# Second attention of a two-layer conditioned sequence model: q stacked by DMA like k, scores of two heads as two row-half matmuls

## The reference, cut to what matters

```python
x_mod = _modulate(_ln(x), shift_msa, scale_msa)      # layer norm, scale and shift by the condition
k, q, v = jnp.split(x_mod @ w_qkv, 3, axis=-1)        # each 256 x 256, seen as 256 tokens x 16 heads x 16
q = q / CH
w = jax.nn.softmax(jnp.einsum('bqhc,bkhc->bhqk', q, k), axis=-1)
y = jnp.einsum('bhqk,bkhc->bqhc', w, v).reshape(B, S, H)
x = x + gate_msa[:, None] * (y @ w_proj + b_proj)
```

## Time and profile before

| | us |
|---|---|
| time, median of two runs | 1826.03 (1824.8 and 1827.25) |
| span of the profiled execution, first to last instruction | 1819.8 |
| what the median has more than this span | 6.2 |

### The profile page before, as it was taken

How to read it: one execution, slowest core, us unless ns; L and a number is a source line. 1 busy time by engine, 2 the same in 40 slices (tenths; PEclk the granted TensorE clock), 3 DMA queues, 4 the chain that set the end, 5 groups by cost and what they waited for, 6 DMA issues and landing times. The chain is left out here.

```text
span 1819.8 us, 46726 instructions
## 1 busy us (share of the span) xinstructions
PE 1757.5 (97%) x15198; PEld 1633.4 (90%) x15198; DVE 1340.7 (74%) x3119; ACT 944.7 (52%) x2099; POOL 362.4 (20%) x470
## 2 busy tenths in 40 slices
PE   7999989999999969999999999999998899999998
PEld 7999989999999967888888888888886899999998
DVE  4888876666666647888888888888885677777776
ACT  2666653333333345777676777777776333333332
POOL 2233331222122200111111111111111212221221
PEclk8999989999999989999999999999999799999999
DMA  7300010000000002111111111111110111111111
GB/s 215 127 20 20 20 33 1 0 0 0 0 0 0 0 14 72 52 49 50 48 48 48 48 48 48 48 48 49 49 49 27 50 47 46 35 46 46 46 42 39
DMA packets 73579, 73.97 MB, mean 41 GB/s; under 512 B 13489, under 2 KB 63985, under 8 KB 73537
## 3 DMA queue, kind: packets, MB, share of 16 engines
q1 hardware_dynamic: 70928, 73.31, 12.9%
q10 hardware_dynamic: 2448, 0.08, 0.1%
q0 software_dynamic: 160, 0.04, 0.0%
HBM read 38.62 MB, written 8.55 MB: 26 GB/s over the span
## 5 line engine op out<-in xcount | busy, mean ns | idle before, releaser
L1418 DVE TENSOR_REDUCE C_negmax<-bank 128x2 f32<-128x512 f32 x512 | 340.2, 686 | 101.1 <-PE bank L1226 98.1
L1338 ACT ACTIVATE C_probs<-bank 128x512 f32<-128x512 f32 x512 | 301.3, 598 | 139.2 <-PE bank L1238 134.4
L1226 PE MATMUL bank<-C_kx,C_qs 128*128 128x256 f32 x1024 | 217.9, 295 | 5.1 <-DMA C_kx<-C_k_hi 2.6
L892 ACT ACTIVATE D_g<-bank,D_bias 128x256 f32<-128x256 f32 x256 | 107.6, 472 | 221.3 <-PE bank L181 221.3
L1238 PE MATMUL bank<-C_qs,C_kx 128*128 128x256 f32 x1024 | 221.2, 298 | 0.1
L892 ACT ACTIVATE B_g<-bank,B_bias 128x256 f32<-128x256 f32 x256 | 107.6, 472 | 218.5 <-PE bank L181 193.1
L1226 PEld LDWEIGHTS bank<-C_kx,C_qs 128*128 128x128 f32 x1024 | 156.2, 189 | 33.3 <-issue 17.7
L1238 PEld LDWEIGHTS bank<-C_qs,C_kx 128*128 128x128 f32 x1024 | 155.9, 189 | 29.0 <-ACT C_probs L1338 15.6
L181 PE MATMUL bank<-D_wt_w_hi,D_g_lo 128*128 128x256 f32 x512 | 147.3, 288 | 6.0 <-DVE D_g_lo L920 4.6
L181 PE MATMUL bank<-B_wt_w_hi,B_g_lo 128*128 128x256 f32 x512 | 145.7, 285 | 5.2 <-DVE B_g_lo L920 5.0
L181 PE MATMUL bank<-B_h_hi,B_wt_w_lo 128*128 128x256 f32 x512 | 147.4, 288 | 1.9 <-DVE B_h_lo L294 1.9
(11 more groups left out here) (265 smaller groups left out, 5218.0 us busy)
## 6 DMA issues: line engine op xcount, KB each, us to landing
C_kx<-C_k_hi SPq DMA_DIRECT2D x256, 64.0 KB, 2.6
C_kx<-C_k_lo SPq DMA_DIRECT2D x128, 64.0 KB, 2.6
C_gbc<-mod_rows SPq DMA_DIRECT2D x32, 256.0 KB, 3.2
D_gbc<-mod_rows SPq DMA_DIRECT2D x32, 256.0 KB, 3.4
out<-xres SPq DMA_DIRECT2D x32, 256.0 KB, 3.5
xres<-in_x SPq DMA_DIRECT2D x4, 1792.0 KB, 16.6
A_orow_bc<-mod_rows SPq DMA_DIRECT2D x32, 128.0 KB, 2.9
stage<-in_L_cond_mlp_w SPq DMA_DIRECT2D x2, 1024.0 KB, 12.5
```

Of the source, the lines that this page charges most:

```text
L892: ins = eng.activation(g[u][:, d * S:(d + 1) * S], hbank[u][:, d * S:(d + 1) * S], func, bias=per_seq(bias1, 2 * u + d, b))
L1226: ins = eng.matmul(sbank[h % 2][:, qh * S:(qh + 1) * S], qs[b.par][:, t * S + qh * P:t * S + (qh + 1) * P], kx[b.par][e][:, t * S:(t + 1) ...
L1338: e_exp.by(eng.activation(probs[h % NP][:, :], stbank[h % 2][:, :], ACT.Exp, scale=scl))
L1418: e_max.by(eng.tensor_reduce(n3[:, :, col], sbank[h % 2][:, :].rearrange("p (q k) -> p q k", q=TH), AX, ALU.max, negate=True))
```

## The change

* q is permuted like k (the weights of q too), and its high and low parts go into qs by DMA: `place` issues 6 DMAs of 64 KB for each half w of the heads, for q as for k. `Q_SLOTS` is (hi, hi, lo), `K_SLOTS` (lo, hi, hi). The selection tiles, SQ0 to SQ3, and the moves on ACT are gone.
* kx is one tile for each parity, with both halves filled; a score matmul reads 48 rows (50 for the transposed scores) of one half. A task is now a pair of heads: 4 matmuls, alternating between the halves and the two banks. A pair waits until both maxima (exponentials) of the pair before are taken.
* q0, k0 wait for lo_q, lo_k; q1 and k1 wait for task v of their sequence. hi_q waits until all 24 DMAs of the sequence before have landed; hi_k no longer waits for DMAs.
* The tables have new slots; PEEL is 6, MAX_SKEW 4, and the first input load keeps its 4 sequences (X_FIRST).

```diff
-PEEL = 4
+PEEL = 6
+X_FIRST = 4
...
-        SLOTS, MAX_SKEW = 16, 3
+        SLOTS, MAX_SKEW = 16, 4
...
-                K_SLOTS = ("hi", "lo", "hi")
-                K_DMAS = 2 * len(K_SLOTS)
...
-                kx = [[sb(f"kx{u}{e}", [P, NT * S], F32R) for e in range(2)] for u in range(UNROLL)]
+                Q_SLOTS, K_SLOTS = ("hi", "hi", "lo"), ("lo", "hi", "hi")
+                ROWS = len(K_SLOTS) * CH
+                STACK_DMAS = 2 * (len(Q_SLOTS) + len(K_SLOTS))
...
+                kx = [sb(f"kx{u}", [P, NT * S], F32R) for u in range(UNROLL)]
...
+                            for n in "qk":
+                                w_raw, s_in = raw_qk[n]
+                                eng.wait_ge(s_in, 16)
...
+                                        ins = eng.tensor_copy(d4, s5[:, :, :, :, e])
...
-                T_PE = {"T": -0.5, "q": 3, "k": 6.5, "v": 16.5, "SQ0": 8.5, "SQ1": 12, "SQ2": 13, "SQ3": 14.5,
-                        "M0": 25.5, "M1": 33, "AV0": 38, "AV1": 41, "AV2": 46.5, "AV3": 49.5, "Y1a": 45, "Y1b": 52,
-                        "Y2": 55, "PR": 59}
...
+                T_PE = {"T": -0.5, "q": 5.5, "k": 8, "v": 16.5, "M0": 26.5, "M1": 34.5, "AV0": 39, "AV1": 42.5,
+                        "Y1a": 47, "AV2": 47.5, "AV3": 51, "Y1b": 54, "Y2": 57, "PR": 61}
+                T_ACT = {"hi_h": 0.5, "hi_q": 6.5, "hi_k": 9, "v": 18, "M0": 27, "M1": 35, "Y0": 43.5, "Y1": 52,
+                         "hi_y": 58}
+                T_DVE = {"stats": -3.5, "xhat": -2, "lo_h": 1.5, "lo_q": 8.5, "lo_k": 10, "M0": 27.5, "M1": 35.5,
+                         "Y1a": 48, "Y1b": 55.5, "lo_y": 59, "out": 62}
...
-                T_S, T_ST = {h: 16 + h for h in range(NH)}, {h: 32.5 + h for h in range(NH)}
...
+                T_S, T_ST = {f"S{t}": 18 + 2 * t for t in PAIRS}, {f"ST{t}": 33.5 + 2 * t for t in PAIRS}
+                T_MAX, T_EXP = {t: T_S[f"S{t}"] + 0.5 for t in PAIRS}, {t: T_ST[f"ST{t}"] + 0.5 for t in PAIRS}
...
-                            e_max.wait(eng, b, h - 1)
+                        def scores(b, t):
+                            if t % 4 == 0:
+                                eng.wait_ge(s_st[t // 4][b.par], (b.pair + 1) * STACK_DMAS * 16)
+                            e_max.wait(eng, b, 2 * t)
                             for qh in range(TH):
...
+                                for e in range(2):
+                                    rows = slice(e * HALF, e * HALF + ROWS)
+                                    ins = eng.matmul(sbank[e][:, qh * S:(qh + 1) * S],
+                                                     qs[b.par][rows, t * S + qh * P:t * S + (qh + 1) * P],
+                                                     kx[b.par][rows, t * S:(t + 1) * S], start=True, stop=True)
+                                    if qh == TH - 1:
+                                        e_s.by(ins)
...
                         def hi_q(b):
-                            e_sq.wait(eng, b.back(1))
-                            hi_bias(b, "q", qk["q_hi"], bias_q, e_q, e_hiq)
-
-                        def hi_k(b):
                             prev = b.back(1)
                             if not prev.before_first():
                                 for w in range(2):
-                                    eng.wait_ge(s_kst[w][prev.par], (prev.pair + 1) * K_DMAS * 16)
+                                    eng.wait_ge(s_st[w][prev.par], (prev.pair + 1) * STACK_DMAS * 16)
+                            hi_bias(b, "q", qk["q_hi"], bias_q, e_q, e_hiq)
...
-                        def place_k(b, w):
...
+                        def place(b, w, name, stacked, slots, e_lo):
...
                             if w == 0:
-                                e_lok.wait(eng, b)
+                                e_lo.wait(eng, b)
                             else:
-                                e_sqev.wait(eng, b)
+                                e_v.wait(eng, b)
                             for e in range(2):
-                                for slot, part in enumerate(K_SLOTS):
+                                for slot, part in enumerate(slots):
...
-                        T_SP = {"k0": 10, "k1": 21.5, "M0": 26, "M1": 38.5, "gates": 41}
...
+                        T_SP = {"q0": 9.5, "k0": 12, "q1": 17.5, "k1": 21, "M0": 28, "M1": 36, "gates": 41}
```

More of the change, by code:

```diff
@@ L231, in stats @@
                 if x_in is not None:
-                    s, dmas = x_in[0 if b.reg is None and b.off < PEEL else 1]
+                    s, dmas = x_in[0 if b.reg is None and b.off < X_FIRST else 1]
                     eng.wait_ge(s, 16 * dmas)
@@ L1117, in _ @@
-                            ins.then_inc(s_mmk, 1)
+                            for n in "qk":
+                                eng.wait_ge(s_perm[n], 1)
+                                for t in range(KT):
+                                    for k in range(KT):
+                                        ins = eng.matmul(pshift[n][:, t * NB:(t + 1) * NB],
+                                                         w_perm[n][:, k * D + t * P:k * D + (t + 1) * P],
+                                                         shift1a[:, k * NB:(k + 1) * NB], start=k == 0, stop=k == KT - 1)
+                                ins.then_inc(s_mmb[n], 1)
@@ new lines, in scores_t @@
+                        def scores_t(b, t):
+                            if t % 4 == 0:
+                                eng.wait_ge(s_mdma[t // 4][b.par], (b.pair + 1) * MAX_DMAS * 16)
+                            e_exp.wait(eng, b, 2 * t)
+                            for kh in range(TH):
+                                for e in range(2):
+                                    rows = slice(e * HALF, e * HALF + ROW_LO + 1)
+                                    ins = eng.matmul(stbank[e][:, kh * S:(kh + 1) * S],
+                                                     kx[b.par][rows, t * S + kh * P:t * S + (kh + 1) * P],
+                                                     qs[b.par][rows, t * S:(t + 1) * S], start=True, stop=True)
+                                    if kh == TH - 1:
+                                        e_st.by(ins)
@@ L1432, in lo_bias, with lo_q, maxima @@
                             e_out.by(ins)
-                        def lo_k(b):
+                        def lo_q(b):
                             e_st.wait(eng, b.back(2), 8)
-                            lo_bias(b, "k", qk["k_hi"], qk["k_lo"], bias_k, e_hik, e_lok)
+                            lo_bias(b, "q", qk["q_hi"], qk["q_lo"], bias_q, e_hiq, e_loq)
+                        def maxima(b, t):
+                            for h in (2 * t, 2 * t + 1):
+                                maximum(b, h)
                         def y_norm(b, w):
```

198 lines of the change are left out of this document (67 added, 131 removed).

## The result

The changed kernel takes 2175.57 us (median of 2174.45 and 2176.69) against 1826.03: 1.191 of the time before, 95% interval 1.188 to 1.195, so 349.5 us slower. The forecast was 1948 us, in a range from 1885 to 2005: the direction was right, the size far off. The profiled execution has a span of 2174.8 us.

What follows compares the result with a forecast made beforehand. PE bounded the kernel before, at 22.41 us a sequence; a circle of waits (25.7 us, plus 0.6 for the clock) would replace it. 31 x (26.3 - 22.41) = 121, plus 1.2 prelude: 1826 + 122 = 1948 us, range 1885 to 2005.

Steps and rivals of the forecast that it cites:

- Step 1: ACT, DVE, SP: hi_q then lo_q end 1.95 us after the last k1 DMA lands; q0, k0 issue from there.
- circle: Waits closing over one sequence, from landed DMAs through hi_q, DVE, v and q1 to the next landing: 25.7 us.
- step 4: DVE: xhat waits for POOL's rstd (0.82 us), then xhat 1.33, out 0.76, maxima of pair 6 1.29.
- Step 6: SP: q1 waits 3.6 us for v, then q1, M1, k1 issues and landing take 11.0 us.
- SP's price: SP: each q DMA issue costs 0.64 us like k's; a half of six with its gap takes 3.93 us.
- rival 4: PE: row halves may not overlap but run one after the other; 6 us each way; no chance given.
- rival 3: PE falls to 1.2 GHz every period, mode changes add: 28 us or more, about 2001 us; chance 0.20.
- Rival 1: PE's relief comes through: a period near 20 us, 1752 us; chance 0.03.

Runs made afterwards that it cites:

- run 2: The changed kernel with POOL's two residual additions taken one iteration sooner; 1940.88 us.
- run 4: The kernel before with MAX_SKEW 4 (and with it POOL's lag), PEEL 6 and `out` moved past stats; 2039.87 us.
- run 3: As run 2, with q1 and k1 no longer waiting for v, and M1 behind k1 on SP; 1874.16 us.
- run 10: As run 6, with q made one place sooner on PE, ahead of the transposed scores of pair 2; 1789.51 us (0.980).
- run 7: The kernel before with row halves alone in the score matmuls, still one head at a time; 1896.68 us (1.040).
- run 5: As run 3, with two copies of q_hi, q_lo, k_hi, k_lo, hi_q waiting for DMAs of two sequences before; 1873.47 us (1.026).
- run 6: As run 5, with xhat behind the maxima of pair 6 on DVE and out, T, hi_h later; 1838.08 us (1.008).
- run 8: As run 5, with DVE's list laid out anew, stats half an iteration earlier; 1883.91 us (1.030).
- run 9: As run 8, but with one copy of q_hi, q_lo, k_hi, k_lo; 1882.94 us (1.029).

## Why the prediction was right or wrong, point by point

* **Step 1 failed**: "q0 and k0 are issued from here". The step looked at the semaphore that q0 waits for, and not at what stands ahead of q0 on SP, the gates load, with a wait of its own on POOL. q0 starts 10.3 us after lo_q's end (1026.16 to 1036.49), not at once. In the first sequences, where the gates load does not wait yet, rstd rows stand at 706.56, 733.08 and 760.73 us, 26.5 and 27.7 apart, where 26.3 was forecast. Run 2 takes POOL's lag away and lands 7 us from the forecast; run 4 puts it with the later `out` into the kernel before and costs 218 us.
* That run 2 lies only 7 us from the forecast is in part luck. Its circle has the forecast's parts: lo_q, M0, the wait at q1, the landing, and the clock at 0.5 in each period (for 3.4 us in most). But 31 steps of 25.75 - 22.41 us give 104 and not 121 us; xhat took 0.73 us where 1.33 was forecast. The fill ahead of the first rstd (668.06 us, before 664.38) and all that comes behind the last (1453.47 of 1939.0 us, before 1345.81 of 1819.8) give some 15 us where 1.2 was forecast for the prelude and nothing for fill and drain.
* Behind step 1 stand two rows of the change that were read as neutral: MAX_SKEW 4, which is also POOL's lag, and `out` "62" behind "stats" and "xhat". The prediction quotes DVE's new order, and in step 4 uses it for a sum of durations, but doesn't ask who takes C_tmp, and when POOL passes.
* **Step 4** also lacked the wait of `out` for POOL, 1.4 us, since rstd and both additions stand one behind the other on POOL. Its 0.82 us for rstd were nearly right (0.91).
* **Step 6**: in the profile after, q1 doesn't wait for v, as SP comes to it so late. In run 2 it does, 3.9 us against 3.6; in run 3 it goes, and 2.1 us of a period with it.
* **SP's price** was right: six issues of q take 3.91 us with the gap behind them (1022.15 to 1026.06 in run 2), as k's took 3.93, and by the profile page after they land 2.5 to 2.6 us behind their issue.
* **Row halves**: rival 4 is out. PE's timeline of run 10:

```profile
1004.76 0.51 PE L1218 MATMUL bank<-C_qs,C_kx 50*128 50x256 f32 x4
1005.11 0.40 PE L1205 MATMUL bank<-C_kx,C_qs 48*128 48x256 f32 x4
1005.44 0.39 PE L180 MATMUL bank<-C_h_hi,C_wq_lo 128*128 128x256 f32 x1
```

  Four matmuls on alternating halves take 0.33 us from their start to the full-height matmul behind them (1005.11 to 1005.44), with 0.1 us for the change of shape in it, where four full-height ones take 0.48 (0.12 each). PE's need is 185.09 us in 200 us of run 10, or 19.2 us a sequence; the forecast took 19. Its "some tenths of a microsecond" for a change of shape were more than its rows said (0.20 - 0.12 = 0.08 us ahead of the products with v); run 7 has 0.1 us on either side.
* **The clock** (rival 3 gave 2001 us for it): after the change PE is at the 1.2 GHz level for 14 to 17 of 34 us in nearly all periods, but as a follower of SP's stall: in run 2, with the gates load in time, it is there for 3.4 us in most periods, and the period is 25.75. What the low clock by itself adds to the 34 us, no run separates. In runs 3, 5, 6, 8 and 9 a fall, behind an idle stretch of 1.3 us where rival 3 had 2.6, makes the sequence in which it comes some 1.4 to 1.5 us longer.
* **Rival 1**, PE's relief, does exist: 1789.5 us in run 10, against 1752 worked out. The way there took four things that the change didn't bring: POOL's addition in time, q1 without v, rstd hidden, and q where PE waited. They were added one on the other, and no run leaves one of the earlier ones out at the end.

## What to carry to other kernels

For a wait on a queue that works in order, list what stands ahead of the instruction too: one small DMA with a wait of its own, which cost nothing while it was always met, can hold up all that is put behind it. When a task is moved past another in one engine's list, look for the engine that takes its output at a fixed point of the iteration: put behind that point, the output is taken an iteration later (30 us here). Where several limits lie close together, opening one may show nothing until the next is found. And a mean period can hide two kinds of sequences: sort them by the granted clock before a gain is put down to the clock.

## What the runs showed of the hardware that was not expected

xhat is the same instruction in all runs, and takes twice as long beside POOL's additions as with POOL at rest. The groups of DVE from 800 to 1300 us (count, busy us, mean ns, idle before), after:

```profile
L268 DVE TENSOR_SCALAR C_xhat<-xres,C_mv,C_rstd 128x256 f32 x28 | 21.6, 809 | 12.0 <-POOL C_rstd L255 12.0
```

and in run 2, where POOL rests during xhat (rstd ends at 1017.30, the next operation starts at 1018.81, xhat runs from 1017.33 to 1018.06):

```profile
L268 DVE TENSOR_SCALAR C_xhat<-xres,C_mv,C_rstd 128x256 f32 x38 | 14.0, 409 | 16.4 <-POOL C_rstd L255 16.4
```

809 against 409 ns; before it was 682, so the kernel before paid a part of this too. POOL's first addition takes 1.46 us for its two instructions beside xhat and 1.42 alone. The Trainium skill, page "SBUF — State Buffer", section "SBUF: two separate sides", says that DVE and GpSimd share one pair of ports, and that a DVE instruction in a 2-port mode (or, against one of GpSimd that reads SBUF, with two SBUF inputs) and a GpSimd instruction lock each other out for the whole of the one that began first. In which mode xhat runs, no run shows; the rows agree in direction: of the two it is DVE's instruction that becomes longer.
